# A two-layer adaLN transformer on one core: where a LayerNorm row block is kept, and where a weight split and a norm stand in their engines' programs

## The reference

```python
h = _layernorm(x) * (1 + ca) + sa
x = x + ga * _L1_attn_ref(h, ...)              # 16 heads of 8, no mask
h = _layernorm(x) * (1 + cb) + sb
# _L1_ffn_ref(h): top-1 of 8 experts
router_probs = softmax(h @ Wr + br); idx = argmax; gates = max
xn = (h - mu) * rsqrt(var + 1e-5) * ln_g + ln_b        # a third LayerNorm, of h
y  = relu(xn @ W1[idx] + b1[idx]) @ W2[idx] + b2[idx]
x = x + gb * y * gates
```

## Time and profile before

| | us |
|---|---|
| median of 3 executions | 939.29 |
| lowest, highest | 934.75, 940.22 |
| the profiled execution: time, span | 939.55, 937.8 |
| PE, DVE, ACT, POOL busy (share of the span) | 777.5 (83%), 645.0 (69%), 533.5 (57%), 247.9 (26%) |
| layer 1's attention, 650 to 700 us: PE, DVE, ACT busy | 45.14, 44.36, 30.47 of 50 |
| sparse blocks, 850 to 875 us: PE, DVE, ACT, POOL busy | 19.73, 22.91, 18.18, 12.15 of 25 |

### The profile page before, as it was taken

The page is one execution under the profiler, slowest core; times in us unless marked ns, Lnnn a source line. Parts: engine busy times, 40 slices in busy tenths (PEclk is TensorE's granted clock), DMA queues, the critical chain, the costliest instruction groups (busy, mean ns, idle before and its releaser), DMA issues. The chain is left out here.

```text
span 937.8 us, 12907 instructions
## 1 busy us (share of the span) xinstructions
PE 777.5 (83%) x4212; PEld 490.8 (52%) x4212; DVE 645.0 (69%) x1292; ACT 533.5 (57%) x976; POOL 247.9 (26%) x327
## 2 busy tenths in 40 slices
PE   5598888888988999999999799989989998238750
PEld 3355445545545777778767444444444452237740
DVE  4475686766653867867867696888988794538933
ACT  2255445555565777776767356656656666027740
POOL 4247654525323000000000230012202321144425
PEclk9599899999999999999999999999999999759985
DMA  6433311111100950000001211311312310021113
GB/s 181 71 69 92 63 35 23 34 41 30 36 2 2 285 163 1 0 1 1 1 12 23 71 32 25 74 41 36 91 24 44 83 25 13 0 85 35 34 35 84
DMA packets 56623, 46.84 MB, mean 50 GB/s; under 512 B 5831, under 2 KB 46620, under 8 KB 56556
## 3 DMA queue, kind: packets, MB, share of 16 engines
q1 hardware_dynamic: 55291, 43.52, 19.6%
q0 software_dynamic: 1120, 2.30, 0.9%
q10 hardware_dynamic: 144, 0.20, 0.1%
HBM read 14.67 MB, written 14.55 MB: 31 GB/s over the span
## 5 line engine op out<-in xcount | busy, mean ns | idle before, releaser
L929 ACT ACTIVATE ring<-single 128x512 f32<-128x512 f32 (+3 forms) x512 | 253.1, 518 | 195.5 <-PE single L1194 185.2
L1583 DVE TENSOR_REDUCE mneg<-pair 128x2 f32<-128x1024 f32 (+3 forms) x256 | 258.3, 1022 | 73.1 <-PE pair L1178 34.6
L1194 PE MATMUL single<-q_op,k_op 128*128 128x512 f32 (+3 forms) x512 | 214.9, 438 | 14.2 <-ACT ring L929 9.1
L1174 PE MATMUL pair<-k_op,q_op 128*128 128x512 f32 (+3 forms) x512 | 167.8, 407 | 17.7 <-DVE mneg L1583 11.2
L1194 PEld LDWEIGHTS single<-q_op,k_op 122*128 122x128 f32 (+1 forms) x512 | 97.0, 195 | 94.9 <-ACT ring L929 72.7
L1174 PEld LDWEIGHTS pair<-k_op,q_op 120*128 120x128 f32 (+1 forms) x512 | 98.0, 203 | 59.2 <-DVE mneg L1583 33.9
L1211 PE MATMUL p_o<-ring,vaug 128*9 128x512 f32 (+3 forms) x1024 | 113.7, 516 | 1.0 <-ACT ring L929 0.9
L1635 DVE TENSOR_TENSOR ring<-ring,single 128x1024 f32<-128x1024 f32 x60 | 73.2, 1221 | 46.0 <-ACT ring L958 44.5
L958 ACT ACTIVATE ring<-pair,cols 128x512 f32<-128x512 f32 x136 | 86.2, 686 | 31.4 <-PE pair L1258 25.7
L1640 DVE TENSOR_TENSOR hid_lo<-ring,hid_hi 128x1024 fp32r<-128x1024 f32 x68 | 83.3, 1225 | 23.1 <-ACT hid_hi L973 19.8
L973 ACT ACTIVATE hid_hi<-ring 128x1024 fp32r<-128x1024 f32 x68 | 72.2, 1061 | 31.3 <-issue 30.2
(11 more groups left out here) (313 smaller groups left out, 1336.3 us busy)
## 6 DMA issues: line engine op xcount, KB each, us to landing
xs<-zero SPq DMA_DIRECT2D x10, 1024.0 KB, 10.3
k_op<-hl SPq DMA_DIRECT2D x112, 64.0 KB
q_op<-hl SPq DMA_DIRECT2D x16, 256.0 KB
stage<-in_L_ffn_W_dram SPq DMA_DIRECT2D x8, 512.0 KB, 4.8
stage<-in_L_ffn_rW_dram SPq DMA_DIRECT2D x6, 512.0 KB, 4.9
q_op<-hl SPq DMA_DIRECT2D x48, 64.0 KB
xb<-xs SPq DMA_DIRECT2D x15, 128.0 KB, 2.1
xs<-yb SPq DMA_DIRECT2D x15, 128.0 KB, 1.7
```

Source lines behind the costliest of these rows:

```text
L929: exp_done.by(act.activation(ring[:, n % 8, lo:T], singles[n % 2][:, lo:T], ACT.Exp), (L, n))
L1174: ins = pe.matmul(both[:, i, 0:hi], r32(qs[:, P * qt:P * (qt + 1)]), r32(ks[:, 0:hi]), start=i == 0 or L == 1 or qt >= 2, stop=L == 1)
L1194: st_full.by(pe.matmul(singles[n % 2][:, lo:T], r32(ks[:, P * kc:P * (kc + 1)]), r32(qs[:, lo:T]), start=True, stop=True), (L, n))
L1583: s_taken.by(dve.tensor_reduce(mneg[:, G % 2, 2 * p:2 * p + 2, qt], both[:, :, 0:hi], axis=AX.X, op=ALU.max, negate=True), (L, m))
```

## The change

Three edits. (1) In the sparse blocks DVE writes the scaled rows back over the PSUM bank that it reads, and the subtraction takes its first operand from there; the SBUF tile `xt` is gone. (2) In layer 1's POOL program the first weight split of s stands behind `modulate(s-1)`. (3) In the drain the third norm's last part "T.he" stands ahead of "T.rk".

```diff
-         "T.ex", "T.m2", "T.m3", "T.rt1", "T.rt2", "T.rk", "T.he"]
+         "T.ex", "T.m2", "T.m3", "T.rt1", "T.rt2", "T.he", "T.rk"]
...
-        xt = put("xt", [P, BLK], at=at_h + 12 * KB)
...
             for s in range(NB, STAGES):
                 add_bias(s)
-                weights1(2 * (s - NB))
                 if s > NB:
                     modulate(s - 1)
+                weights1(2 * (s - NB))
                 weights1(2 * (s - NB) + 1)
                 if s > NB:
                     scatter(s - 1)
...
-                    step(dve.tensor_scalar(xt[:, :], singles[0][:, 0:BLK], cols[:, R_LNG:R_LNG + 1],
+                    step(dve.tensor_scalar(singles[0][:, 0:BLK], singles[0][:, 0:BLK], cols[:, R_LNG:R_LNG + 1],
                                            cols[:, R_LNB:R_LNB + 1], ALU.mult, ALU.add))
-                    xl_ready.by(dve.tensor_tensor(r32(xt_lo[:, n % 2, :]), xt[:, :], xt_hi[:, n % 2, :], ALU.subtract), n)
+                    xl_ready.by(dve.tensor_tensor(r32(xt_lo[:, n % 2, :]), singles[0][:, 0:BLK], xt_hi[:, n % 2, :], ALU.subtract), n)
```

## The result

| | before | after |
|---|---|---|
| executions, device us | 938.47 median (934.75 to 940.52, 19) | 928.57 median (924.59 to 935.38, 19) |
| profiled execution | 939.55, span 937.8 | 935.38, span 933.7 |

The ratio of after to before is 0.9909, 95% interval 0.9891 to 0.9927: 8.5 us shorter by the ratio (6.9 to 10.2), 9.9 by the two medians. The forecast was 932.0 us; by the ratio the change is just under the line of 1% that the prediction drew.

What follows compares the result with a forecast made beforehand. DVE instructions with two SBUF operands wait for POOL on the path, in the sparse blocks and layer 1's attention. -2.45 - 6.30 + 2.10 - 0.60 = -7.25 us, forecast 932.0 us, range 928.0 to 937.5.

Steps and rivals of the forecast that it cites:

- rival A: Layer 1's last pass, s = 7: POOL does not hold the four-element seed; -9.35 us in all, 929.9 us; chance 20%.
- Edit 1, forecast -2.45: Sparse blocks: subtraction from PSUM no longer waits for POOL's cast; two blocks take 8.61 instead of 9.10 us, five times.
- rival D: Sparse blocks: in-place write to PSUM much slower, say 3.0 us; +11.6 us in all, 951 us; chance 4%.
- rival B: Sparse blocks: subtraction from PSUM still held, or hid_lo takes over the wait; -4.8 us in all, 934.5 us; chance 8%.
- Edit 2, the two stalls, forecast -6.30: Layer 1's attention, s = 5 and 6: Newton step no longer held by POOL's weight split; 3.15 us gained per stall.
- the lower bound of 4.1 us: Layer 1's two removed stalls: 2 x 2.05 us of waiting, if DVE's other work fills part of the gap.
- rival C: Layer 1: each removed stall gives only 2.05 us, the new hold costs 3.15; -4.0 us in all, 935.3; chance 11%.
- Edit 2, the new hold, forecast +2.10: Layer 1, s = 7: the moved weight split holds DVE's four-element seed until POOL's subtraction ends, costing 2.1 us.
- The bound of 3.15: Layer 1, s = 7: upper bound in us for the price of the seed's new hold, as the old stalls.
- The narrow call for s = 5: Layer 1, s = 5: POOL's lengthened block ends near 644.67, less than 0.1 us ahead of DVE's next two-SBUF-operand instruction.
- Edit 3, forecast -0.60: Drain: the norm fills DVE's 0.70 us wait for PE's ranks; POOL's scatter is released at 820.05 instead of 820.65.
- The warning at the end of the prediction: Layer 1: the sum is wrong if a removed stall's time returns as PE waiting for DVE's maxima; no size given.

Runs made afterwards that it cites:

- e1_psum: Only the sparse blocks' in-place scaling and subtraction from PSUM, put into the kernel before: median 936.39 us, ratio 0.9981 to the kernel before.
- e3_norm: Only the drain's third norm moved ahead of the ranks, put into the kernel before: median 936.20 us, ratio 0.9984 to the kernel before.
- e10: The changed kernel with POOL's sparse weight cast released earlier, right behind hid_lo; last pass's first split still behind modulate: median 925.11 us, ratio 0.9869 to the kernel before.

## Why the prediction was right where it was, and wrong where it was not

The mechanism of each edit was as predicted, and the time lies in the range, 3.4 us under the forecast. But 928.57 is not in the forecast's own range of 930 to 934; as a number it comes nearer to rival A's 929.9, whose mechanism is out. Of the 3.4, 0.8 are the base: the forecast was made against a median of 939.29, all nineteen executions have 938.47. Some 1.2 are terms that were sized too small, as below. The rest, 1.4, is that the medians lie 9.9 us apart where the ratio, and the means of the same executions, give 8.5.

- **Edit 1, forecast -2.45.** Right, in cause and size. Every second cast follows in 8.60 us instead of 9.10, from the first `yt` to the last it is 2.31 us, the new limit is the end of the weight cast, and e1_psum alone gives 1.8 us (0.1 to 3.6). `hid_lo` met the cast in two of fifteen blocks (1.56 and 1.53 us against 1.23), the few tenths that the prediction had left in its range. The in-place write to PSUM costs 11 ns an instruction (546 against 535), so rival D had nothing under it. L1674 at 0.425 us rules out rival B.
- **Edit 2, the two stalls, forecast -6.30.** The mechanism was right, the term mis-sized: between these two traces it measures -7.2. The starts of DVE's `mT` step (L1516 before, L1515 after), seven of them here, show how the lead of the changed kernel grows, in us:

| `mT` before | after | lead |
|---|---|---|
| 599.14 | 601.05 | -1.91 |
| 615.55 | 615.39 | 0.16 |
| 633.66 | 632.10 | 1.56 |
| 666.90 | 665.31 | 1.59 |
| 683.39 | 679.65 | 3.74 |
| 701.69 | 696.38 | 5.31 |
| 764.96 | 759.56 | 5.40 |

The first stall is worth 2.07 us up to the next `mT` and 1.40 up to the one behind it; the second 2.15 and 1.57; together 7.19, and nothing moves between them or after. The first part is the hold. The second is PE at a lower clock, and it lasts longer than I counted. I had taken ACT's idle time at 618.42, 4.39 - 1.24 = 3.15, but the clock was still down behind that row, as this window of the kernel before shows:

```profile
618.00:622.00 4.00, 3.92 (x21) 2.02 (x21) 2.68 (x6) 2.02 (x4) 0.00 (x0) 0.89 0.36 66
```

A stall has to be read between two marks well outside it. That the second part is the clock's, e1_psum shows. Its first stall is if anything longer (2.38 us, and PE waits 2.61 for `mT`), but the clock stays at 1.00 behind it:

```profile
616.83 1.16 PE L1097 MATMUL p_m<-w_oga,oT 128*128 128x128 f32 x8 [2.61 <-DVE mT L1515]
```
```profile
614.00:618.00 4.00, 1.39 (x10) 1.17 (x10) 3.83 (x9) 0.85 (x3) 1.01 (x1) 1.00 0.00 0
618.00:622.00 4.00, 3.92 (x22) 2.06 (x22) 3.79 (x8) 2.44 (x5) 0.00 (x0) 1.00 0.37 70
```

There the next `mT` comes 2.2 us late and the one behind it no later still: 33.31 us over the two steps, 31.05 without a stall (after), 34.52 in the kernel before and 34.72 in e3_norm, where the clock fell. The second stall cost 3.7 us in all three traces that have it, with a fall each time. So the lower bound of 4.1 us holds only if the clock never falls, and rival C, whose price for the new hold was 3.15 as well, is out by the time.
- **Edit 2, the new hold, forecast +2.10.** Right in place, instruction and length (L1405 at 2.12 us, in s = 7 only), so rival A is out. Its price is 1.5 us with the clock at 1.00 (2.0 by the whole pass of e10), as PE idles for less than the hold lasts; with the clock falling the pass is 4.6 to 6.3 us longer. The bound of 3.15 was too low. I knew from the earlier trace rows that a stall can take the clock with it; the bound had that at the old stalls' size, the forecast had none of it. The narrow call for s = 5 came true: POOL's moved block ends at 643.08, and DVE's next instruction with two SBUF operands (L1524) starts at 643.18, free by 0.10 us.
- **Edit 3, forecast -0.60.** 0.85 by the traces. The norm starts 0.09 us behind the start of DVE's cast L1552 and the rank 1.03 us behind the norm's start (817.03 to 818.06); I had started the one behind the other's end. Each overlaps the one before by 0.08 to 0.09 us here, and two of these made the 0.2. (The prediction's 820.05 should read 820.03; it changes nothing.)
- **The sum.** With what was measured: -2.4 - 7.2 + 1.5 to 2.0 - 0.85 = -8.5 to -9.0, against 8.5 us by the ratio (6.9 to 10.2). That is agreement within the interval and no closer: with e1's first stall it would be 1.2 less, and each execution in which the clock falls in s = 7 loses 2.5 to 4.3 more. In the profiled execution the last pass takes 2.6 us more than in e10 for the clock, and the start-up, the same work in both, took 1.91 us longer (the first row of the table of `mT`); that is why this execution shows only 4.1 us less of span.

The warning at the end of the prediction, that a removed stall's time could come back as waiting for maxima, did not come true: the stretch to s = 6 is 63.25 before and 63.16 after.

## What to carry to other kernels

When an instruction lasts many times what its size explains, look for the other engine's instruction that ends with it: either move one operand to PSUM or let one engine wait for the other's end, which here took 0.20 us off every two blocks by adding a wait. A block of POOL work that is moved takes its hold along, so follow it to what DVE issues under it in every pass, the last one included. Read the worth of a stall between two marks far apart, and look at the granted clock behind a stall before trusting one profiled execution with its price.

## What the runs showed of the hardware that I had not expected

- The same hold and the same idle time of PE (1.45 and 1.46 us, 3.35 of 5 us busy) were followed by a granted clock near 0.50 for 10 us in one trace and by 1.00 in another. Of the four traced holds in s = 7 three show a fall, of the six traced stalls of the Newton step five. What the executions outside the profile pay on average (1.7 us, plus or minus 1.4) fits the trace without one, and can't say how often the clock falls.
- A TENSOR_SCALAR on 128x4 elements with one SBUF operand is held like one with two (2.12 us against 0.17). The Trainium skill (VectorE: DVE Perf Modes, section "What auto-detection actually checks") counts a single source and a destination in SBUF, with outer dimensions that are even or equal, as the condition of a two-port mode; that fits, though no run here shows the mode itself.
- DVE works in place on PSUM at nearly the price of PSUM to SBUF: 546 ns against 535 for 128x256.
